# An attention stage with 1024 softmax reciprocals moved to 128 partitions by DMA, and a new order of TensorE's side work

## What is computed

```python
qkv = X @ W_qkv
qkv = qkv.reshape(b, s, h, d, 3)
q, k, v = (qkv[..., 0], qkv[..., 1], qkv[..., 2])
scores = jnp.einsum('bqhd,bkhd->bhqk', q, k) / scale
weights = jax.nn.softmax(scores, axis=-1)
attn = jnp.einsum('bhqk,bkhd->bqhd', weights, v)
return attn.reshape(b, s, h * d) @ W_out
```

## Time and profile before

| | us | of the span |
|---|---|---|
| median of 3 runs | 1840.99 | |
| the profiled execution, its own time | 1841.47 | |
| its span | 1839.6 | |
| PE busy | 1727.4 | 94% |
| DVE busy | 1547.9 | 84% |
| ACT busy | 1459.2 | 79% |
| POOL busy | 1444.4 | 79% |

### The profile page before, as it was taken

The page is one execution under the profiler, slowest core; times in us unless marked ns, Lnnn a source line. Parts: engine busy times, 40 slices in busy tenths (PEclk is TensorE's granted clock), DMA queues, the critical chain, the costliest instruction groups (busy, mean ns, idle before and its releaser), DMA issues. The chain is left out here.

```text
span 1839.6 us, 32373 instructions
## 1 busy us (share of the span) xinstructions
PE 1727.4 (94%) x9247; PEld 924.8 (50%) x9247; DVE 1547.9 (84%) x2180; ACT 1459.2 (79%) x1954; POOL 1444.4 (79%) x869
## 2 busy tenths in 40 slices
PE   5899999999999999999999999999999899975687
PEld 5444444444444444444444444444444677763456
DVE  7888888888888888888888888888888878888886
ACT  4488888888888888888888888888888777864553
POOL 5388888888888888888888888888888256654664
PEclk9899999999999999999999999999999999997899
DMA  7212121212212121212122121212122777331000
GB/s 258 79 36 80 36 80 46 80 46 69 78 52 86 34 80 36 80 46 80 46 69 82 51 83 34 80 36 80 46 80 62 241 218 218 115 99 48 0 18 29
DMA packets 125334, 143.31 MB, mean 78 GB/s; under 512 B 26737, under 2 KB 106673, under 8 KB 122098
## 3 DMA queue, kind: packets, MB, share of 16 engines
q1 hardware_dynamic: 120306, 132.61, 23.6%
q0 software_dynamic: 4992, 10.27, 1.7%
HBM read 87.20 MB, written 27.64 MB: 62 GB/s over the span
## 5 line engine op out<-in xcount | busy, mean ns | idle before, releaser
L1562 POOL TENSOR_TENSOR psum_k<-psum_k,probs 128x1024 f32<-128x1024 f32 x384 | 929.3, 2420 | 103.9 <-ACT probs L1499 83.8
L1499 ACT ACTIVATE probs<-ps_s 128x1024 f32<-128x1024 f32 x512 | 497.0, 1024 | 149.9 <-PE ps_s L1319 149.9
L1328 PE MATMUL ps_v<-probs,V 128*64 128x512 f32 x2056 | 497.8, 605 | 0.0
L1581 DVE TENSOR_REDUCE mxh<-ps_three 128x2 f32<-128x1024 f32 x264 | 318.5, 1207 | 98.3 <-PE ps_three L1286 98.2
L1483 ACT ACTIVATE ps_s<-peak 128x1024 f32<-128x1024 f32 x224 | 245.1, 1132 | 0.0
L1483 ACT ACTIVATE ps_s<-qkv_raw 128x1024 f32<-128x1024 f32 x224 | 245.0, 1131 | 0.0
L1622 DVE RECIPROCAL e_y_row<-e_y_row 128x128 f32<-128x128 f32 x256 | 241.0, 941 | 0.0
L1328 PEld LDWEIGHTS ps_v<-probs,V 128*64 128x64 f32 x2056 | 124.8, 136 | 228.6 <-issue 209.7
L1319 PE MATMUL ps_s<-e_ew 64*128 64x512 f32 x1536 | 199.0, 391 | 0.0
L1562 POOL TENSOR_TENSOR psum_k<-probs 128x1024 f32<-128x1024 f32 x64 | 152.8, 2388 | 47.2 <-ACT probs L1499 39.4
L854 POOL DMA_INDIRECT results<-e_y_row,e_y_at x92 | 102.6, 1115 | 82.0 <-ACT e_y_row L795 52.8
(11 more groups left out here) (320 smaller groups left out, 3184.4 us busy)
## 6 DMA issues: line engine op xcount, KB each, us to landing
e_ew<-w_split SPq DMA_DIRECT2D x23, 1024.0 KB
qkv_raw<-peaks SPq DMA_DIRECT2D x33, 512.0 KB, 3.9
V<-e_x_raw SPq DMA_DIRECT2D x33, 512.0 KB, 3.6
peak<-peaks SPq DMA_DIRECT2D x32, 512.0 KB, 4.3
xs_hi<-xh SPq DMA_DIRECT2D x16, 512.0 KB, 4.0
xs_lo<-xl SPq DMA_DIRECT2D x16, 512.0 KB, 5.0
rows<-in_blank_d SPq DMA_DIRECT2D x4, 1483.5 KB, 16.9
e_x_raw<-rows SPq DMA_DIRECT2D x23, 258.0 KB
```

Of the source, the lines that this page charges most:

```text
L1328: ins = nc.tensor.matmul(ps_v[rows, :], V[par][:, kt, rows], probs[:, t % RING, x, :], start=kt == 0, stop=kt == KT - 1)
L1499: nc.scalar.activation(probs[:, t % RING, :, :], ps_s[t % 2][:, :, :], ACT.Exp, scale=SCALE).then_inc(p_done, 1)
L1562: nc.gpsimd.tensor_tensor(acc, probs[:, (t - 1) % RING, :, :] if kt == 1 else acc, probs[:, t % RING, :, :], ALU.add).then_inc(add_done, 1)
L1581: nc.vector.tensor_reduce(mxh[:, kh, t, :], max_bank(unit, i)[:, :, :], AX.X, ALU.max).then_inc(m_done, 1)
```

## The change

1. `inverse` works on 128 partitions by 8 words instead of 4 times 128 by 128. After ScalarE has read `den`, SyncE moves one row of 512 of each head to `flat_den` (`flatten`, two DMAs), VectorE does one RECIPROCAL, SyncE stores it to `shares` in HBM (`inverse_out`) and reads it back, one row to 64 partitions for each head (`inverse_back`, two DMAs). `half_pair` puts these in front of and between the two DMAs of `spread`.
2. The visits are put in another order, the two halves of a pair are now alike, and VectorE's program is one function `half`. The denominators come in the first and fifth visit, the outputs in the second and sixth, V in the fourth and last.
3. In visits of `FRONT` the item goes in front of the second product.
4. VectorE's second seed is step 11 instead of 13; `stage` moves from the sixth visit to the fifth and GpSimd's part of it from behind step 11 to behind step 9; a semaphore of the prologue is merged with another.

The diff, cut to its core:

```diff
-    VISIT = [("K1",), ("Q0", "den1"), ("out0",), ("V0",), ("Q1", "den0"), ("out1",), ("V1",), ("K0",)]
+    VISIT = [("Q0", "den1"), ("out0",), ("K1",), ("V0",), ("Q1", "den0"), ("out1",), ("K0",), ("V1",)]
-    BY_V = (3, 13)
+    BY_V = (3, 11)
...
+            def flatten(n, hf):
+                sp.wait_ge(xa_done, reads(n, f"den{hf}"))
+                for x in range(2):
+                    sp.dma_start(flat_den[x * DH:(x + 1) * DH, :], den[x * DH:x * DH + 1, :].rearrange("a (c k) -> a c k", c=DH)).then_inc(inv_moved, 16)
+            def inverse_out(k):
+                sp.wait_ge(inv_done, k + 1)
+                sp.dma_start(g.shares[:, :].rearrange("a (c k) -> (a c) k", c=DH), flat_inv[:, :]).then_inc(inv_moved, 16)
+            def inverse_back(k):
+                sp.wait_ge(inv_moved, inv_moved_out(k))
+                for x in range(2):
+                    sp.dma_start(rden[x * DH:(x + 1) * DH, :], g.shares[x:x + 1, :].to_broadcast([DH, CH])).then_inc(inv_moved, 16)
+            def half_pair(n, unit, hf):
+                k = n * 2 + 1 - hf
+                flatten(n, hf)
+                inverse_out(k)
+                spread(unit, hf)
+                inverse_back(k)
+                spread_back(unit, hf)
...
                     if p in SHARED:
                         row_max_shared(n, t, i, other, unit % 2)
                     else:
+                        item(n, par, VISIT[p][0], b)
                         row_max(n * 2 + unit, i, other, unit % 2)
-                        item(n, par, VISIT[p][0], b)
...
-            def inverse(n, hf, part):
-                cols = slice(part * P, (part + 1) * P)
-                v.wait_ge(xa_done, reads(n, f"den{hf}"))
-                ins = nc.vector.reciprocal(rden[:, cols], den[:, cols])
+            def inverse(n, hf):
+                v.wait_ge(inv_moved, flat_moved(n * 2 + 1 - hf))
+                nc.vector.reciprocal(flat_inv[:, :], flat_den[:, :]).then_inc(inv_done, 1)
...
+                def half(hf, late, early, par):
+                    t = KT - KT * hf
+                    step(t)
+                    step(t + 1)
+                    low(n, early, nxt)
+                    seed(n, t + 3)
+                    row_max_upper(n, t + 2)
+                    row_max_lower(n, t + 2)
+                    row_max_shared(n, t + 3)
+                    inverse(n, hf)
+                    add_out(n, f"out{1 - hf}")
+                    step(t + 4)
+                    step(t + 5)
+                    low(n, late, par)
+                    if hf:
+                        expert_part(n)
+                    row_max_upper(n, t + 6)
+                    row_max_lower(n, t + 6)
+                    row_max_shared(n, t + 7)
+                    normalise(n, hf)
+                half(1, "K1", "Q0", nxt)
+                half(0, "K0", "Q1", par)
```

More of the change, by code:

```diff
@@ L997, in layer0_attention @@
     PRESETS = 3
-    LATE_PRESETS = 5
+    ONES_PRESETS = 4
+    LATE_PRESETS = 6
     HEADS = [slice(x * DH, (x + 1) * DH) for x in range(2)]
@@ L1012, in layer0_attention @@
     warm = sb("warm", [P, 1], F32)
+    flat_den = sb("flat_den", [P, 2 * CH // P], F32)
+    flat_inv = sb("flat_inv", [P, 2 * CH // P], F32)
     x_rows = sb("x_rows", [P, 2, ROW], F32)
@@ L1060, in layer0_attention @@
     xv_done = sem("xv_done")
-    rden_done = sem("rden_done")
+    inv_done = sem("inv_done")
+    inv_moved = sem("inv_moved")
     picked = sem("picked")
@@ L1142, in upper, with flat_moved, inv_moved_out, inv_moved_back @@
         return n * len(SHARED) + SHARED.index(t // 2) + 1
+    def flat_moved(k):
+        return k * 80 + 32
+    def inv_moved_out(k):
+        return k * 80 + 48
+    def inv_moved_back(k):
+        return k * 80 + 80
     def chunk(name):
@@ L1189, in _ @@
                 sp.dma_start(xs_lo[:, :].bitcast(F32), g.xl[:, batch].bitcast(F32)).then_inc(xs_in, 16)
-                spread(n * 2 + 1, 1)
+                half_pair(n, n * 2 + 1, 1)
                 expert_part(n)
                 load_part(n + 1)
-                spread(n * 2 + 2, 0)
-                spread(n * 2 + 3, 1)
+                half_pair(n, n * 2 + 2, 0)
+                half_pair(n + 1, n * 2 + 3, 1)
                 expert_part(n + 1)
                 load_part((n + 2) % N)
-                spread(n * 2 + 4, 0)
+                half_pair(n + 1, n * 2 + 4, 0)
                 sp.wait_ge(xa_done, reads(n + 1, "V1"))
@@ L1200, in _ @@
             sp.wait_ge(peak_in, (N * 2 + 1) * 16)
+            sp.wait_ge(inv_moved, inv_moved_back(N * 2 - 1))
             sp.wait_ge(we_in, (N + 1) * 16)
@@ L1358, in _ @@
             pe.wait_ge(picks_done, 1)
-            pe.wait_ge(ones_n_done, 1)
+            pe.wait_ge(preset, ONES_PRESETS)
             for k, left in enumerate((g.before, ones_n)):
@@ L1502, in _ @@
                     if p not in SHARED:
-                        read(n, VISIT[p][0], par if p == VISITS - 1 else 1 - par)
+                        read(n, VISIT[p][0], par if VISIT[p][0] == "K0" else 1 - par)
                     for k in (t + 1, t + 2):
@@ L1517, in _ @@
                         read(n, name, 1 - par)
-                    if p == 5:
+                    if p == VISITS // 2:
                         stage(n)
@@ L1565, in _ @@
                         scatter(hf)
-                    if t != STEPS - 5:
+                    if t != STEPS - 7:
                         continue
```

19 lines of the change are left out of this document (8 added, 11 removed).

## The result

The changed kernel is slower: 1861.65 us (median of 4 runs, 1859.03 to 1868.28) beside 1840.16 us of the kernel before on the same chip; the ratio is 1.0118, 95% interval 1.009 to 1.0145. The prediction was 1830. The profiled execution took 1859.03 us with a span of 1857.2.

A forecast was written before the change was run, and what follows sets the result against it. TensorE, busy 298.47 of 300 us, was taken as the bound. Savings of 0.96 us a pair (30.7 us), less 19.2 given back in even pairs, took 1841.47 to 1830.0 us; range 1808 to 1862.

The forecast's parts named there:

- second rival: TensorE's extra step beside each projection costs 0.43 us on both sides instead of 0.32: 28 more, 1858 us; chance 0.12.
- F - 5.35: How long VectorE's reciprocal, awaiting flattened words, holds TensorE in the K visit; F counts from den visit's end E.
- The middle that I took, 6.4: First half of even pairs: flattened words land 6.4 us after den visit's end, between 5.7 and 7.1.
- The visits would be 5.87 with den (3.14 + 716.68 - 713.95): Den visits: 3.14 us from start to values, plus the old trace's distance from values to den's end.
- Nothing for these: Other work: ScalarE and GpSimd have room, `stage` and GpSimd's low part move into idle time; priced at nothing.
- fourth rival: No change, 1841 us: something the additions only covered holds V visits, such as upper maximum behind K's low part; chance 0.13.
- the price of an even pair: First half of even pairs: the late flattening gives back 1.2 us a pair, 19.2 us over 16 pairs.
- The hold of 1.05: Even pairs: VectorE, waiting for the flattened words, holds TensorE's second product of the K visit by 1.05 us.
- the 0.15 for late seeds: Even pairs: maxima reach ScalarE's seeds late behind the moved DMAs, leaving some 0.15 us on TensorE.
- VectorE is late because it has eight reciprocals: VectorE's row: eight 942 ns reciprocals, 7.5 us a pair, make it late; it counts only where TensorE waited.
- the 0.06 a visit for projections in front: Projection visits: projection before the second product removes a wait but adds a step, saving 0.23 us a pair over four visits.
- third rival: The DMA chain becomes the bound at ScalarE's seeds of steps 8 and 0, waiting for `peak`: 1862 us; chance 0.10.

The follow-up runs named there:

- the kernel of ratio 0.9826: Changed kernel with Q's low part before the second maximum, xs loads earlier, expert subtraction in the second half, and reciprocals back on VectorE without DMAs: 1797.04 us, ratio 0.9826.
- all three edits: Changed kernel with Q's low part before the second maximum, xs loads half a pair earlier, expert subtraction in the second half: 1805.40 us, ratio 0.9831.

## Why the prediction was wrong

**What held.** Scores to projection took 0.32 (the projection starts 1.82 after the visit, 1.49 + 0.33), values 3.15 (forecast 3.14), V visits 4.84 (4.82), out 4.78 (4.83), K 5.03 (5.01); the second rival had no ground. In odd pairs and second halves the DMA chain is hidden, as said. F, the moment at which the flattened words can be used, came at E + 5.83, between the ends 5.7 and 7.1, and by the formula F - 5.35 holds K1 by 0.48; it is 0.55. The middle that I took, 6.4, was too late, and my reason for the early end doesn't hold up. The Trainium skill (DMA: Bandwidth & Descriptors, Anatomy of one DMA) calls HBM the heaviest target for the receipt of a write, from which I had 5.7 for a write to SBUF. Here the flattening into SBUF landed after 1.7 us at the least and 1.8 in the median, and the 4 KB store of the inverses to HBM after 1.4 in every one of 64 cases, so the receipt's target is not what the trace shows.

**The step that failed first: "The visits would be 5.87 with den (3.14 + 716.68 - 713.95)".** I copied the distance from the values to the end of den from the old order, 2.73, and did not ask what den waits for. `bank_free` needs the low part of Q, and the order that I printed puts it behind a maximum whose product I had myself moved 0.89 us later (from 1.83 to 1.87 after the start to 2.72). 0.36 x 64 = 23 us: with it alone the forecast would have been 1853, slower than before. The row was at hand: `low` (L1616 before) in VectorE's timeline beside the start of den. The sentence "Nothing for these" covered ScalarE, GpSimd and `stage`, and no sentence put a price on VectorE's low part of Q; the fourth rival names a low part, but that of K in the V visits.

**The step that failed second: the price of an even pair.** The hold of 1.05 was too large (0.55), and the 0.15 for late seeds (0.25 by the prediction's own terms) came to nothing. The list of what is behind the reciprocal on VectorE was too short: addition and maximum stood in it, and the subtraction a few places further did not; before, it took 0.64 us in the median. Pushed back by the late reciprocal, it ran into GpSimd's addition, and 1.37 came on top. 1.92 instead of 1.2, 16 times, is 11.5 us. Together 23 + 11.5 = 34.5, less 32 x 0.1, is 31; the profiled execution took 1859.03 - 1830.0 = 29 more. The 0.1 is a slip inside the sum: the forecast's own visits add up to 41.06 and it used 41.15, in part because V1's item stood 0.23 late, 741.76 - 739.66 = 2.10 behind its values against 1.87, and not 0.17.

**What was credited wrongly.** "VectorE is late because it has eight reciprocals": without them the old order gains 0.1% (0.999), and with them the new one loses nothing (0.9826). The V visits are at 4.82 to 4.84 with all eight reciprocals in the row (the kernel of ratio 0.9826), so their forecast gain doesn't need the reciprocals gone; what is left of the change for it is the additions' new place. And the 0.06 a visit for projections in front was their worth in the old order; with the additions in front of the first maximum it is 0.37 in each K visit and 0.09 in each out visit, and without them the order with all three edits takes 41.97 us a pair (reads from 79.0 to 1421.9) instead of 41.00, nearly what the kernel before took.

The second and third rival had the right sign with the wrong mechanism. The third named the DMA chain at ScalarE's seeds, which waited less than 1 us in the whole span; the chain did its harm on VectorE's row. That the third rival's 1862 is the time measured is luck.

## What to carry to other kernels

When a product is moved back in a row, follow each of its readers to everything behind them: what frees the bank may be an instruction that does not read the product at all. An operation with a wait, put in the middle of another engine's row, must be costed with all that stands behind it until the next idle time, and the durations of two-input operations in SBUF are not constants: look at their shortest and longest before moving them against GpSimd. A busy share that falls by 13 points, as VectorE's did here, says nothing about time: ask first where the work stands.

## What the runs showed of the hardware

- A VectorE subtraction of 128x256 with both inputs in SBUF took 0.42 us free and up to 2.28 when it began inside one of GpSimd's additions; the 15 long ones of the change ended 0.28 us after that addition, and those of the kernel before and of the changed kernel with the reciprocals back ended 0.28 to 0.29 after it. A multiplication of 128x512 took 0.68 against 2.19 (median) and 2.36, ending 0.55 after the addition. What such an instruction costs is set by how much of the addition is left when it begins. The kernel before already paid: its `normalise` took 1.26 to 1.78, and its subtraction 0.64 (median).
- A RECIPROCAL of 128x8 takes 0.203 us and one of 128x128 0.942: an estimate of (942 - 203) / 120 = 6.2 ns a column, if the time grows evenly with the width.
- The small DMA from SBUF to SBUF (2 KB, 8 words to a partition) landed after 1.7/1.8/5.4 us (shortest, median, longest), the 4 KB store of the inverses to HBM after 1.4 each time, the read-back of 128 KB after 2.7/3.5/4.2. Issued behind 512 KB loads, the flattened words could be used 4.2 us after the issue of the first began (681.05 to 685.25).
